# Last stage of a fused four-layer kernel: products turned through VectorE and DRAM in place of TensorE

## The chip, the cores and the metric

The kernel runs on one core of a Trainium2 chip. The metric is the device time of one execution in microseconds, the median of several runs. One further execution was profiled; its trace is what the sections below read.

## The reference

The input x is (16, 128, 512) float32, 2048 rows of 512. Four layers follow one another, each `x = x + tanh(g) * f(layernorm(x))`: a latent cross attention, a feed-forward with routed low-rank parts, a causal attention, and last the layer that the change touches:

```python
h = relu(x @ W1 + b1)
alpha = softmax(h @ W2 + b2)              # 8 weights for each row
vx = einsum('krd,bsd->bskr', V, x)        # 8 x 64 = 512 columns
uvx = einsum('kdr,bskr->bskd', U, vx)
out = einsum('bsk,bskd->bsd', alpha, uvx)
```

All is computed in float32. The products of the last layer are split into a high and a low half (hi, lo) of the type fp32r, and each is three matmuls: lo x hi, hi x lo, hi x hi.

## The kernel before

The rows are worked in four blocks m = 0 to 3 of 512 rows, each of four tiles tb of 128 rows. Every engine runs its own program, written out by hand in the order in which it is to run (functions `tensor`, `scalar`, `vector`, `gpsimd`, `sync`), and the engines meet at semaphores only. An engine that waits holds back all that stands behind it in its program. All transfers are issued from SyncE's program. A function of the same name (`ln_turn`, `out4`, ...) stands in several programs and is the part of that engine in one step.

The steps of the last stage, for block m:

- `h4`: four groups of 12 matmuls, the first layer of the weights. It needs the turned and split rows of the whole block. ScalarE drains each with Relu to H4.
- `logits_a`, `logits_b`: 8 + 8 small matmuls, with a copy by ScalarE (LT) between them; VectorE and ScalarE make the softmax weights `al` of the block.
- `vx4(m, tb)`: 12 matmuls give the 512 columns of vx for a tile. VectorE multiplies them by the weights into VX, which has two buffers.
- `turn4(m, tb)`: four transposes of VX on TensorE (128x128 each, by a product with the identity) into a PSUM bank; ScalarE writes the high half and VectorE the low half to VT4, two buffers.
- `out4(m, tb)`: 12 matmuls by U; VectorE multiplies by tanh(g) and adds x, which lies in X4 (eight buffers); SyncE stores the tile.
- `ln_turn(3, m+1, tb)`: four transposes of the normalised rows of the next block, then the high half by ScalarE and the low half by VectorE. `ln_pre` (statistics, VectorE), the reciprocal root (GpSimd) and `ln_norm` (VectorE) precede it.

TensorE's order in block m before is: h4(m), out4(m-1, 2), logits_a, out4(m-1, 3), logits_b, ln_turn(3, m+1, 0), then for tb = 0 to 4: vx4(m, tb), turn4(m, tb-1), ln_turn(3, m+1, tb), out4(m, tb-2). So behind the last ln_turn of a block stand out4(m, 1) and turn4(m, 3), and then h4(m+1). In block 0 there is no out4 ahead and ln_turn(3, 1, 0) stands in the loop. The rows of the next block are loaded once into X4, where the statistics read them and the sum of out4 is formed later; `ln_norm` writes the normalised rows to XR, a ring of five buffers.

The first stage already turns its attention weights in the way that the change uses: VectorE transposes 32x32 blocks from Pb to PY, SyncE stores PY to a DRAM buffer (`p_store`) and loads it back with the blocks in their places (`p_load`, four loads), then ScalarE and VectorE split it.

Names in the profile go by the memory that a tile lies in: P is P3 (H4, VX), PTV is X4, MSK is LT, AR or XT is the turned rows (XT in even blocks, AR in odd ones) and AR is VT4 and the weights. L118 is a matmul, L121 a transpose on TensorE, L124 an operation of ScalarE, L130 a tensor-tensor and L137 a tensor-scalar one on VectorE, L140 the scaled sum, L164 VectorE's 32x32 transpose, L170 a transfer.

Of the kernel before, what the change touches and what calls it, by code (L numbers as in the profile page):

```python
# [180 lines left out]
def build(nc, i, out):  # L181
    ctx = ExitStack()
    with ctx:
# [123 lines left out]
        VX = P3[:, 1, 0:1024].rearrange("p (b n) -> p b n", b=2)  # L307
        VT4 = ar(0, 2048).rearrange("p (b n) -> p b n", b=2)
# [4 lines left out]
        scr = [nc.dram_tensor(f"scr{k}", [NT, D], F32, kind="Internal").ap() for k in range(3)]  # L313
        pscr = [nc.dram_tensor(f"pscr{k}", [128, 1024], F32, kind="Internal").ap() for k in range(2)]
# [31 lines left out]
        t_py, d_pz = sig("t_py", 16), sig("d_pz", 16)  # L346

# [8 lines left out]
        py_ok, pz_ok = kinds(on_dve, "py_ok pz_ok")  # L356
# [170 lines left out]
        def tensor(pe):  # L527
# [537 lines left out]
            def out4(m, tb):  # L1065
                k = ps.take(("o4", m, tb), ring8.next())
                pe.wait_ge(*ps.free(("o4", m, tb)))
                pe.wait_ge(*ps.drained(("vt", m, tb)))
                pe.wait_ge(*w4_ok["U", 3])
                for c in range(4):  # L1070
                    s, s2 = slice(128 * c, 128 * c + 128), slice(512 + 128 * c, 640 + 128 * c)
                    ins = mm3(k[:, :], (VT4[:, tb % 2, s], VT4[:, tb % 2, s2]), (h3(U4[0], c), h3(U4[1], c)), c == 0, c == 3)
                ins.then_inc(*ps.fill(("o4", m, tb)))

            for m in range(NM):
                more = m + 1 < NM
                if m:
                    h4(m, range(4), ring8)
                    out4(m - 1, 2)
                    logits_a(m)  # L1080
                    out4(m - 1, 3)
                    logits_b(m)
                    if more:
                        ln_turn(3, m + 1, 0, ring8.next())
                for tb in range(5):
                    if tb < 4:
                        vx4(m, tb)
                    if tb >= 1:
                        turn4(m, tb - 1)
                    if more and tb < 4 and (tb >= 1 or m == 0):  # L1090
                        ln_turn(3, m + 1, tb, ring8.next())
                    if 2 <= tb < 4:
                        out4(m, tb - 2)
# [4 lines left out]
        def scalar(ac):  # L1098
# [340 lines left out]

            for m in range(NM):  # L1440
                more = m + 1 < NM
                if m:
                    h4(m, range(4))
                logits(m)
                if m and more:
                    ln_turn(3, m + 1, 0)
                ac.wait_ge(*al_in[m])
                ac.act(al[:, :, :], al[:, :, :], ACT.Exp).then_inc(*al_ex.mark(m))
                for tb in range(5):
                    if tb >= 1:  # L1450
                        turn4(m, tb - 1)
                    if more and tb < 4 and (tb >= 1 or m == 0):
                        ln_turn(3, m + 1, tb)


        def vector(ve_):
# [6 lines left out]
            def ln_pre(ph, m, tb):  # L1463
                par = (4 * ph + m) % 2
                if ph == 3 and m:
                    x = X4[:, 4 * (m % 2) + tb, :]
                    e.wait_ge(*d_x4[4 * (m % 2) + tb][m])
                else:
                    x = xr_ap("ln", ph, m, tb)
                    e.wait_ge(*xr_ld("ln", ph, m, tb))  # L1470
                e.bn_stats(st6[:, tb, :], x).then_inc(*on_dve.step())
                e.wait_ge(*on_dve.now())
                e.bn_aggr(mv[:, par, tb, :], st6[:, tb, :]).then_inc(*on_dve.step())
                e.wait_ge(*on_dve.now())
                e.ts(ve[:, par, tb:tb + 1], mv[:, par, tb, 1:2], EPS, None, ALU.add, None).then_inc(*ve_ok.mark((ph, m, tb)))

            def ln_norm(ph, m, tb):
                par = (4 * ph + m) % 2
                o = xr_ap("ln", ph, m, tb)
                x = X4[:, 4 * (m % 2) + tb, :] if ph == 3 and m else o  # L1480
                e.wait_ge(*rs_ok[ph, m, tb])
                if ph == 3 and m:
                    e.wait_ge(*xr_free("ln", ph, m, tb))
                e.ts(o, x, mv[:, par, tb, 0:1], rstd[:, par, tb:tb + 1], ALU.subtract,
                     ALU.mult).then_inc(*xn_ok.mark((ph, m, tb)))
# [431 lines left out]
            def vx4(m, tb, a):  # L1917
                key = "vx", m, tb
                t = 4 * m + tb
                e.wait_ge(*ps.full(key))  # L1920
                e.wait_ge(*a)
                e.wait_ge(*(ps.full(("vt", (t - 2) // 4, (t - 2) % 4)) if t >= 2 else ps.full(("pt3", 15, 3))))
                e.tt(VX[:, tb % 2, :].rearrange("p (k r) -> p k r", k=8), ps.ap(key)[:, :].rearrange("p (k r) -> p k r", k=8),
                     bc(al[:, tb, :], 64), ALU.mult).then_inc(*ps.drain(key, on_dve))

# [15 lines left out]
            for m in range(NM):  # L1941
                more = m + 1 < NM
                if more and m:
                    ln_pre(3, m + 1, 0)
                    ln_pre(3, m + 1, 1)
                    ln_norm(3, m + 1, 0)
                    ln_norm(3, m + 1, 1)
                if m:
                    out4(m - 1, 2)
                    out4(m - 1, 3)  # L1950
                    a = logits(m)
                    if more:
                        ln_turn(3, m + 1, 0)
                if m == 0:
                    ln_pre(3, 1, 0)
                    ln_pre(3, 1, 1)
                for tb in range(5):
                    if more and tb < 4 and (tb >= 2 or m == 0):
                        ln_norm(3, m + 1, tb)
                    if tb < 4:  # L1960
                        vx4(m, tb, a)
                    if tb >= 1:
                        turn4(m, tb - 1)
                    if more and tb < 4 and (tb >= 1 or m == 0):
# [3 lines left out]
                    if 2 <= tb < 4:  # L1968
# [170 lines left out]
        def sync(e):  # L2139
# [210 lines left out]
            xf_load(3, 3)  # L2350
            x4_load(1)
# [8 lines left out]
            x4_load(0)  # L2360
            for m in range(NM):
                if m and m + 1 < NM:
                    n = 4 * ((m + 1) % 2)
                    for tb in (0, 1):
                        e.wait_ge(*t_x4[n + tb][m - 1])
                        e.wait_ge(*stored(3, m + 1, tb))
                        e.dma(X4[:, n + tb, :], rows(3, m + 1, tb)).then_inc(*d_x4[n + tb].mark(m + 1))
                if m:
                    x4_store(m - 1, 2)
                    x4_store(m - 1, 3)  # L2370
                if m and m + 1 < NM:
                    n = 4 * ((m + 1) % 2)
                    for tb in (2, 3):
                        e.wait_ge(*t_x4[n + tb][m - 1])
                        e.wait_ge(*stored(3, m + 1, tb))
                        e.dma(X4[:, n + tb, :], rows(3, m + 1, tb)).then_inc(*d_x4[n + tb].mark(m + 1))
                x4_store(m, 0)
                x4_store(m, 1)
# [109 lines left out]
```

## Time and profile before

| | us |
|---|---|
| median of 3 runs (lowest, highest) | 1394.04 (1393.75, 1394.27) |
| the profiled execution | 1391.57 |
| its span, first to last instruction | 1389.8 |
| mean granted clock of TensorE | 0.996 |

PE is TensorE's matmuls and PEld its weight loads, which overlap them. DVE is VectorE, ACT ScalarE, POOL GpSimd, SPq the transfers as SyncE issues them. A row of the timeline gives the start, the duration, the engine, the line, the operation, the tile written and the tiles read, and in brackets how long the engine had been idle and who released it. The duration of a matmul or of an operation of VectorE or ScalarE includes its pipeline, so that the next one on the engine starts before the end. The last stage, from the first vx4 on, runs from 1246 us to the end of the span.

### The profile page before, as it was taken

The page shows a single profiled execution, that of the slowest core. Times are in us where ns is not written, and L with a number is a line of the kernel's source. Part 1 is how long each engine was busy: PE and PEld are TensorE (multiplying, and loading weights), DVE is VectorE, ACT ScalarE, POOL GpSimd, SP SyncE. Part 2 cuts the span into 40 slices and gives each one's busy share as a digit, 9 for nine tenths or more (in the row PEclk, how much of TensorE's full clock was granted, in tenths as well). Part 3 has the DMA queues.
Part 4 walks back from the last instruction along what each step waited for, and adds up shares of the span by engine and source line. Part 5 has one row for each costly group of instructions (what it writes and reads, how often), then busy time and mean ns, then how long its engine had stood idle before and what let it go on. Part 6 is the DMA issues. An engine that isn't in the chain of part 4 may idle for free.

```text
span 1389.8 us, 20437 instructions
## 1 busy us (share of the span) xinstructions
PE 1360.6 (98%) x7708; PEld 1103.3 (79%) x7708; DVE 906.3 (65%) x1759; ACT 518.9 (37%) x1569; POOL 416.0 (30%) x463
## 2 busy tenths in 40 slices
PE   7899999999999999999999999999999999999999
PEld 5688888888788788878887888788886788878887
DVE  5566565666674777786677657776888777834443
ACT  2444455454464232231113111311127777712221
POOL 3112423223254352111120111013518865530000
PEclk9999999999999999999999999999999999999999
DMA  7643444433444222110111101111224031131111
GB/s 264 185 153 114 149 124 129 144 107 119 154 147 111 80 76 57 54 38 20 31 46 31 42 23 45 36 46 56 80 82 137 33 114 62 58 116 57 53 46 46
DMA packets 86726, 120.51 MB, mean 87 GB/s; under 512 B 10444, under 2 KB 49484, under 8 KB 86628
## 3 DMA queue, kind: packets, MB, share of 16 engines
q1 hardware_dynamic: 86628, 119.21, 27.4%
q8 instruction: 61, 1.00, 0.3%
q14 instruction: 37, 0.30, 0.1%
HBM read 86.67 MB, written 32.51 MB: 86 GB/s over the span
## 4 chain that ended last, share of the span: by engine, by line
PE 88%; DVE 7%; ACT 2%; DMA 1%; issue 1%; POOL 1%; SPq 1%; DVEq 0%; ACTq 0%
PE bank L118 84%; PE bank L121 5%; DVE XR L140 1%; ACT Pb L124 1%; DVE STG L130 1%; DVE AH L130 1%; SPq L170 1%; DMA PYZ<-pscr 1%; DVE PYZ L164 0%; DVE XR L137 0%; DVE st L152 0%; ACT STG L124 0%; DVE sm L146 0%; DVE AH L127 0%; DMA XR<-in_x_dram 0%
## 5 line engine op out<-in xcount | busy, mean ns | idle before, releaser
L118 PE MATMUL bank<-XT,AR 128*128 128x512 f32 x1152 | 280.2, 393 | 0.3 <-DVE AR L130 0.2
L118 PE MATMUL bank<-AR 128*128 128x512 f32 x1056 | 262.3, 397 | 5.8 <-DVE Msb L127 4.9
L118 PEld LDWEIGHTS bank<-XT,AR 128*128 128x128 f32 x1152 | 213.8, 188 | 48.4 <-issue 1.5
L118 PEld LDWEIGHTS bank<-AR 128*128 128x128 f32 x1056 | 193.7, 188 | 52.2 <-DVE Msb L127 5.3
L124 ACT ACTIVATE STG<-bank,b1c 128x512 f32<-128x512 f32 x128 | 88.4, 690 | 379.1 <-PE bank L118 302.7
L118 PE MATMUL bank<-AR,CT 128*128 128x512 f32 x768 | 194.2, 396 | 1.8 <-DVE CT L130 1.8
L118 PE MATMUL bank<-AR,AH 128*128 128x512 f32 x768 | 187.6, 391 | 0.0
L127 DVE CAST AH<-STG 128x512 fp32r<-128x512 f32 x192 | 90.5, 471 | 120.9 <-PE bank L118 106.6
L118 PEld LDWEIGHTS bank<-AR,AH 128*128 128x128 f32 x768 | 143.0, 188 | 30.4 <-issue 1.1
L118 PEld LDWEIGHTS bank<-AR,CT 128*128 128x128 f32 x768 | 141.1, 190 | 30.1 <-DVE CT L130 2.5
L127 POOL CAST BA<-STG 128x256 fp32r<-128x256 f32 x64 | 29.7, 464 | 422.2 <-PE bank L118 321.1
L130 DVE TENSOR_TENSOR AH<-STG,AH 128x512 fp32r<-128x512 f32 x192 | 142.6, 743 | 6.6
L124 ACT ACTIVATE Pb<-bank,sm 128x128 f32<-128x128 f32 x256 | 90.1, 377 | 118.0 <-DVE sm L136 118.0
L130 POOL TENSOR_TENSOR Pb<-Pb,sm 128x512 f32<-128x512 f32 x64 | 66.6, 1042 | 189.5 <-DVE sm L149 189.5
L118 PE MATMUL bank<-TM,BA 128*128 128x512 f32 x384 | 107.7, 392 | 0.5 <-ACT STG L124 0.4
L124 ACT ACTIVATE P<-bank,sm 128x128 f32<-128x128 f32 x256 | 90.1, 395 | 31.9 <-DVE sm L146 31.9
L130 POOL TENSOR_TENSOR rstd<-ve,mhalf 128x1 f32<-128x1 f32 x64 | 48.1, 755 | 170.3 <-DVE ve L136 170.2
L118 PE MATMUL bank<-AH,BA 128*128 128x512 f32 x384 | 98.0, 390 | 0.0
L130 DVE TENSOR_TENSOR STG<-STG 128x512 f32<-128x512 f32 x128 | 89.9, 702 | 4.2
L130 POOL TENSOR_TENSOR P<-P,sm 128x512 f32<-128x512 f32 x64 | 65.4, 1042 | 82.1 <-DVE sm L149 82.0
L124 ACT ACTIVATE AR<-bank 128x512 fp32r<-128x512 f32 x88 | 51.7, 603 | 100.2 <-PE bank L121 75.2
L118 PEld LDWEIGHTS bank<-TM,BA 128*128 128x128 f32 x384 | 71.3, 188 | 17.6 <-ACT STG L124 2.2
(135 smaller groups left out, 1860.1 us busy)
## 6 DMA issues: line engine op xcount, KB each, us to landing
pscr<-PYZ SPq DMA_DIRECT2D x30, 512.0 KB, 2.9
PYZ<-pscr SPq DMA_DIRECT2D x120, 128.0 KB, 3.0
XR<-scr SPq DMA_DIRECT2D x52, 256.0 KB, 2.8
XR<-in_x_dram SPq DMA_DIRECT2D x32, 256.0 KB, 4.0
scr<-XR SPq DMA_DIRECT2D x32, 256.0 KB, 2.7
STG<-in_Wq_dram SPq DMA_DIRECT2D x8, 512.0 KB, 5.4
STG<-in_WoT_dram SPq DMA_DIRECT2D x8, 512.0 KB, 6.1
STG<-in_W1L_dram SPq DMA_DIRECT2D x16, 256.0 KB, 2.6
```

The source lines that it names most:

```text
L118: return self.e.matmul(o, w, x, start=start, stop=stop, skip_group_check=True) if self.e else Nothing()
L121: return self.e.transpose(o, x, ident) if self.e else Nothing()
L124: return self.e.activation(o, x, func, **kw) if self.e else Nothing()
L127: return self.e.tensor_copy(o, x) if self.e else Nothing()
L130: return self.e.tensor_tensor(out=o, in0=a, in1=b, op=op) if self.e else Nothing()
L140: return self.e.scalar_tensor_tensor(out=o, in0=a, scalar=s, in1=b, op0=op0, op1=op1) if self.e else Nothing()
L170: return self.e.dma_start(o, x) if self.e else Nothing()
```

## The change

In blocks 0 to 2 the weighted products are no longer turned by TensorE. VectorE transposes their 32x32 blocks into a new buffer VY (`blocks4`), SyncE stores the tile to DRAM (`v_store`) and loads it back into XF with the blocks in their places (`v_back`, four loads of 64 KB), and ScalarE and VectorE split it from there to VT4 (`split4`). The four out4 of a block now stand in the next block: behind h4, between logits_a and logits_b, and the last two behind ln_turn(3, m+1, 0). The splits stand in the programs of ScalarE and VectorE between the other steps of that block. Block 3 keeps turn4. The rows of the blocks 1 to 3 are loaded twice, into XR for the layer norm and into X4 for the sum, and `ln_norm` works in place in XR.

```diff
--- before.py
+++ after.py
@@ -305,12 +305,14 @@
         U4 = (ar(14336, 2048), ar(16384, 2048))
         E4 = (ar(18432, 2048), ar(20480, 2048))
         VX = P3[:, 1, 0:1024].rearrange("p (b n) -> p b n", b=2)
+        VY = P3[:, 1, 1024:2048].rearrange("p (b n) -> p b n", b=2)
         VT4 = ar(0, 2048).rearrange("p (b n) -> p b n", b=2)
         H4 = P3[:, 0, :].rearrange("p (c n) -> p c n", c=4)
         X4 = PTV[:, :].rearrange("p (n d) -> p n d", n=8)
         LT = MSK[:, 0, :]
 
         scr = [nc.dram_tensor(f"scr{k}", [NT, D], F32, kind="Internal").ap() for k in range(3)]
+        vscr = [nc.dram_tensor(f"vscr{k}", [128, 512], F32, kind="Internal").ap() for k in range(2)]
         pscr = [nc.dram_tensor(f"pscr{k}", [128, 1024], F32, kind="Internal").ap() for k in range(2)]
         xs = [i["x"], scr[0], scr[1], scr[2], out]
 
...
@@ -1065,7 +1069,7 @@
             def out4(m, tb):
                 k = ps.take(("o4", m, tb), ring8.next())
                 pe.wait_ge(*ps.free(("o4", m, tb)))
-                pe.wait_ge(*ps.drained(("vt", m, tb)))
+                pe.wait_ge(*(vz_ok[m, tb] if m < 3 else ps.drained(("vt", m, tb))))
                 pe.wait_ge(*w4_ok["U", 3])
                 for c in range(4):
                     s, s2 = slice(128 * c, 128 * c + 128), slice(512 + 128 * c, 640 + 128 * c)
@@ -1076,20 +1080,22 @@
                 more = m + 1 < NM
                 if m:
                     h4(m, range(4), ring8)
-                    out4(m - 1, 2)
+                    out4(m - 1, 0)
                     logits_a(m)
-                    out4(m - 1, 3)
+                    out4(m - 1, 1)
                     logits_b(m)
                     if more:
                         ln_turn(3, m + 1, 0, ring8.next())
-                for tb in range(5):
+                    out4(m - 1, 2)
+                    out4(m - 1, 3)
+                for tb in range(4 if more else 5):
                     if tb < 4:
                         vx4(m, tb)
-                    if tb >= 1:
+                    if not more and tb >= 1:
                         turn4(m, tb - 1)
-                    if more and tb < 4 and (tb >= 1 or m == 0):
+                    if more and (tb >= 1 or m == 0):
                         ln_turn(3, m + 1, tb, ring8.next())
-                    if 2 <= tb < 4:
+                    if not more and 2 <= tb < 4:
                         out4(m, tb - 2)
             out4(NM - 1, 2)
             out4(NM - 1, 3)
@@ -1437,19 +1443,33 @@
                 ac.wait_ge(*(ps.full(("o4", (t - 2) // 4, (t - 2) % 4)) if t >= 2 else ps.full(("w3", 3, 3))))
                 hi_of(key, VT4[:, tb % 2, 0:512], ps.ap(key)[:, :])
 
+            def split4(m, tb):
+                t = 4 * m + tb
+                ac.wait_ge(*d_vz[tb][m, 3])
+                ac.wait_ge(*(ps.full(("o4", (t - 2) // 4, (t - 2) % 4)) if t >= 2 else ps.full(("w3", 3, 3))))
+                hi_of(("vz", m, tb), VT4[:, tb % 2, 0:512].rearrange("p (n j c) -> p n j c", n=4, j=4),
+                      XF[:, tb, :].rearrange("p (j n c) -> p n j c", j=4, n=4))
+
             for m in range(NM):
                 more = m + 1 < NM
                 if m:
-                    h4(m, range(4))
+                    split4(m - 1, 0)
+                    h4(m, (0, 1))
+                    split4(m - 1, 1)
+                    h4(m, (2, 3))
                 logits(m)
                 if m and more:
                     ln_turn(3, m + 1, 0)
+                if m:
+                    split4(m - 1, 2)
                 ac.wait_ge(*al_in[m])
                 ac.act(al[:, :, :], al[:, :, :], ACT.Exp).then_inc(*al_ex.mark(m))
-                for tb in range(5):
-                    if tb >= 1:
+                if m:
+                    split4(m - 1, 3)
+                for tb in range(4 if more else 5):
+                    if not more and tb >= 1:
                         turn4(m, tb - 1)
-                    if more and tb < 4 and (tb >= 1 or m == 0):
+                    if more and (tb >= 1 or m == 0):
                         ln_turn(3, m + 1, tb)
 
 
@@ -1462,12 +1482,8 @@
 
             def ln_pre(ph, m, tb):
                 par = (4 * ph + m) % 2
-                if ph == 3 and m:
-                    x = X4[:, 4 * (m % 2) + tb, :]
-                    e.wait_ge(*d_x4[4 * (m % 2) + tb][m])
-                else:
-                    x = xr_ap("ln", ph, m, tb)
-                    e.wait_ge(*xr_ld("ln", ph, m, tb))
+                x = xr_ap("ln", ph, m, tb)
+                e.wait_ge(*xr_ld("ln", ph, m, tb))
                 e.bn_stats(st6[:, tb, :], x).then_inc(*on_dve.step())
                 e.wait_ge(*on_dve.now())
                 e.bn_aggr(mv[:, par, tb, :], st6[:, tb, :]).then_inc(*on_dve.step())
@@ -1477,11 +1493,8 @@
             def ln_norm(ph, m, tb):
                 par = (4 * ph + m) % 2
                 o = xr_ap("ln", ph, m, tb)
-                x = X4[:, 4 * (m % 2) + tb, :] if ph == 3 and m else o
                 e.wait_ge(*rs_ok[ph, m, tb])
-                if ph == 3 and m:
-                    e.wait_ge(*xr_free("ln", ph, m, tb))
-                e.ts(o, x, mv[:, par, tb, 0:1], rstd[:, par, tb:tb + 1], ALU.subtract,
+                e.ts(o, o, mv[:, par, tb, 0:1], rstd[:, par, tb:tb + 1], ALU.subtract,
                      ALU.mult).then_inc(*xn_ok.mark((ph, m, tb)))
 
             def ln_turn(ph, m, tb):
@@ -1919,9 +1932,23 @@
                 t = 4 * m + tb
                 e.wait_ge(*ps.full(key))
                 e.wait_ge(*a)
-                e.wait_ge(*(ps.full(("vt", (t - 2) // 4, (t - 2) % 4)) if t >= 2 else ps.full(("pt3", 15, 3))))
+                if t >= 14:
+                    e.wait_ge(*ps.full(("vt", 3, tb - 2)))
+                else:
+                    e.wait_ge(*(vy_ok[(t - 2) // 4, (t - 2) % 4] if t >= 2 else ps.full(("pt3", 15, 3))))
                 e.tt(VX[:, tb % 2, :].rearrange("p (k r) -> p k r", k=8), ps.ap(key)[:, :].rearrange("p (k r) -> p k r", k=8),
                      bc(al[:, tb, :], 64), ALU.mult).then_inc(*ps.drain(key, on_dve))
+
+            def blocks4(m, tb):
+                t = 4 * m + tb
+                e.wait_ge(*ps.drained(("vx", m, tb)))
+                e.wait_ge(*(t_vy[tb % 2][t - 2] if t >= 2 else ps.full(("pt3", 15, 3))))
+                e.turn(blocks_out(VY[:, tb % 2, :]), blocks_in(VX[:, tb % 2, :])).then_inc(*vy_ok.mark((m, tb)))
+
+            def split4(m, tb):
+                lo_of(("vz", m, tb), VT4[:, tb % 2, 512:1024].rearrange("p (n j c) -> p n j c", n=4, j=4),
+                      XF[:, tb, :].rearrange("p (j n c) -> p n j c", j=4, n=4),
+                      VT4[:, tb % 2, 0:512].rearrange("p (n j c) -> p n j c", n=4, j=4)).then_inc(*vz_ok.mark((m, tb)))
 
             def turn4(m, tb):
                 key = "vt", m, tb
@@ -1940,32 +1967,40 @@
                 final3(3, b)
             for m in range(NM):
                 more = m + 1 < NM
-                if more and m:
-                    ln_pre(3, m + 1, 0)
-                    ln_pre(3, m + 1, 1)
-                    ln_norm(3, m + 1, 0)
-                    ln_norm(3, m + 1, 1)
                 if m:
-                    out4(m - 1, 2)
-                    out4(m - 1, 3)
+                    split4(m - 1, 0)
+                    split4(m - 1, 1)
+                    if more:
+                        ln_pre(3, m + 1, 0)
+                        ln_pre(3, m + 1, 1)
+                        ln_norm(3, m + 1, 0)
+                        ln_norm(3, m + 1, 1)
+                    out4(m - 1, 0)
+                    split4(m - 1, 2)
+                    out4(m - 1, 1)
                     a = logits(m)
                     if more:
                         ln_turn(3, m + 1, 0)
+                    split4(m - 1, 3)
+                    out4(m - 1, 2)
+                    out4(m - 1, 3)
                 if m == 0:
                     ln_pre(3, 1, 0)
                     ln_pre(3, 1, 1)
-                for tb in range(5):
-                    if more and tb < 4 and (tb >= 2 or m == 0):
+                for tb in range(4 if more else 5):
+                    if more and (tb >= 2 or m == 0):
                         ln_norm(3, m + 1, tb)
                     if tb < 4:
                         vx4(m, tb, a)
-                    if tb >= 1:
+                    if more:
+                        blocks4(m, tb)
+                    elif tb >= 1:
                         turn4(m, tb - 1)
-                    if more and tb < 4 and (tb >= 1 or m == 0):
+                    if more and (tb >= 1 or m == 0):
                         ln_turn(3, m + 1, tb)
                     if more and tb < 2:
                         ln_pre(3, m + 1, tb + 2)
-                    if 2 <= tb < 4:
+                    if not more and 2 <= tb < 4:
                         out4(m, tb - 2)
             out4(NM - 1, 2)
             out4(NM - 1, 3)
@@ -2348,6 +2383,8 @@
                 for block in wo_at(u):
                     xf_store(*block)
             xf_load(3, 3)
+            for tb in range(4):
+                ln_load(3, 1, tb)
             x4_load(1)
             for tb in range(4):
                 xf_store(3, tb)
@@ -2358,24 +2395,45 @@
                 e.dma(rows(4, m, tb), X4[:, n, :]).then_inc(*t_x4[n].mark(m))
 
             x4_load(0)
+
+            def v_store(m, tb):
+                t = 4 * m + tb
+                e.wait_ge(*vy_ok[m, tb])
+                if t >= 2:
+                    e.wait_ge(*d_vz[(t - 2) % 4][(t - 2) // 4, 3])
+                e.dma(vscr[tb % 2], VY[:, tb % 2, :]).then_inc(*t_vy[tb % 2].mark(t))
+
+            def v_back(m, tb):
+                t = 4 * m + tb
+                e.wait_ge(*t_vy[tb % 2][t])
+                e.wait_ge(*(vz_ok[m - 1, tb] if m else t_xf[tb][3]))
+                src = vscr[tb % 2].rearrange("(j r) (i x) -> i r j x", j=4, i=4)
+                for k in range(4):
+                    e.dma(XF[32 * k:32 * k + 32, tb, :].rearrange("r (j x) -> r j x", j=4), src[k]).then_inc(
+                        *d_vz[tb].mark((m, k)))
+
             for m in range(NM):
-                if m and m + 1 < NM:
-                    n = 4 * ((m + 1) % 2)
-                    for tb in (0, 1):
-                        e.wait_ge(*t_x4[n + tb][m - 1])
-                        e.wait_ge(*stored(3, m + 1, tb))
-                        e.dma(X4[:, n + tb, :], rows(3, m + 1, tb)).then_inc(*d_x4[n + tb].mark(m + 1))
+                more = m + 1 < NM
+                if m and more:
+                    for tb in range(4):
+                        ln_load(3, m + 1, tb)
                 if m:
-                    x4_store(m - 1, 2)
-                    x4_store(m - 1, 3)
-                if m and m + 1 < NM:
-                    n = 4 * ((m + 1) % 2)
-                    for tb in (2, 3):
-                        e.wait_ge(*t_x4[n + tb][m - 1])
-                        e.wait_ge(*stored(3, m + 1, tb))
-                        e.dma(X4[:, n + tb, :], rows(3, m + 1, tb)).then_inc(*d_x4[n + tb].mark(m + 1))
-                x4_store(m, 0)
-                x4_store(m, 1)
+                    for tb in range(4):
+                        n = 4 * ((m - 1) % 2) + tb
+                        x4_store(m - 1, tb)
+                        if more:
+                            e.wait_ge(*t_x4[n][m - 1])
+                            e.wait_ge(*stored(3, m + 1, tb))
+                            e.dma(X4[:, n, :], rows(3, m + 1, tb)).then_inc(*d_x4[n].mark(m + 1))
+                if more:
+                    for tb in range(4):
+                        v_store(m, tb)
+                        if tb:
+                            v_back(m, tb - 1)
+                    v_back(m, 3)
+                else:
+                    x4_store(m, 0)
+                    x4_store(m, 1)
             x4_store(NM - 1, 2)
             x4_store(NM - 1, 3)
             for n in range(8):
```

The signals and counters that the new steps use (`t_vy`, `d_vz`, `vy_ok`, `vz_ok`) are declared where the dots stand.

## Rows read from the trace of the kernel before

**Rows 1.** The page: busy time, share of the span and instructions of each engine.
```profile
PE 1360.6 (98%) x7708; PEld 1103.3 (79%) x7708; DVE 906.3 (65%) x1759; ACT 518.9 (37%) x1569; POOL 416.0 (30%) x463
```

**Rows 2.** Busy time in two windows: blocks 0 and 1; PEclk is the granted clock.
```profile
1246.00:1267.00 21.00, 20.34 (x105) 16.71 (x104) 14.19 (x29) 3.89 (x7) 2.91 (x4) 1.00 0.23 78
1267.00:1305.60 38.60, 38.60 (x197) 31.41 (x195) 17.94 (x39) 7.94 (x14) 2.67 (x4) 1.00 0.17 56
```

**Rows 3.** Waits from 1246 to 1345: us in total, times, longest.
```profile
PE bank L121 <- DVE XR L137: 0.7, 1, 0.7
```

**Rows 4.** The chain that ended last: start, us; turn4(1, 2) and ln_turn(3, 2, 3).
```profile
1301.77 0.87 PE bank L121 x8
```

**Rows 5.** Timeline, end of block 1: vx4(1, 3), ln_turn(3, 2, 3), h4(2).
```profile
1301.81 0.69 DVE L130 TENSOR_TENSOR P<-bank,al 128x512 f32<-128x512 f32 x1 [1.52 <-PE bank L118]
...
1302.05 0.60 PE L121 MATMUL bank<-ident,XR 128*128 128x128 f32 x4
...
1302.74 0.59 ACT L124 ACTIVATE XT<-bank 128x512 fp32r<-128x512 f32 x1
...
1303.49 0.68 DVE L130 TENSOR_TENSOR XT<-bank,XT 128x512 fp32r<-128x512 f32 x1
...
1305.58 1.41 PE L118 MATMUL bank<-XT,AR 128*128 128x512 f32 x5
```

**Rows 6.** Timeline, block 1: out4(0, 3), ln_turn(3, 2, 0) and the softmax weights.
```profile
1285.08 0.75 DVE L140 SCALAR_TENSOR_TENSOR PTV<-bank,tg,PTV 128x512 f32<-128x512 f32 x1 [3.20 <-PE bank L118]
...
1285.62 0.64 PE L121 MATMUL bank<-ident,XR 128*128 128x128 f32 x4
1285.80 0.19 DVE L130 TENSOR_TENSOR al<-bank,b 128x32 f32<-128x32 f32 x1
...
1286.25 0.19 DVE L130 TENSOR_TENSOR al<-al,s 128x32 f32<-128x32 f32 x1
1286.29 0.60 ACT L124 ACTIVATE XT<-bank 128x512 fp32r<-128x512 f32 x1 [3.61 <-PE bank L121]
1286.79 0.22 ACT L124 ACTIVATE al<-al 128x32 f32<-128x32 f32 x1
...
1287.58 0.68 DVE L130 TENSOR_TENSOR XT<-bank,XT 128x512 fp32r<-128x512 f32 x1
```

**Rows 7.** Timeline, blocks 0 and 1: vx4(0, 1), the norms, turn4(0, 0).
```profile
1250.28 3.00 PE L118 MATMUL bank<-AR,XT 128*128 128x512 f32 x12
...
1252.80 0.54 DVE L137 TENSOR_SCALAR XR<-PTV,mv,rstd 128x512 f32<-128x512 f32 x1
...
1253.12 0.60 PE L121 MATMUL bank<-ident,P 128*128 128x128 f32 x4
...
1293.43 0.68 DVE L130 TENSOR_TENSOR XT<-bank,XT 128x512 fp32r<-128x512 f32 x1
1294.03 0.68 DVE L152 BATCH_NORM_STATS2 st<-PTV 128x6 f32<-128x512 f32 x1
...
1295.04 0.54 DVE L137 TENSOR_SCALAR XR<-PTV,mv,rstd 128x512 f32<-128x512 f32 x1
```

**Rows 8.** Line 137, norms in place: ns min/median/max, first and last start.
```profile
L137 DVE TENSOR_SCALAR XR<-XR,mv,rstd x36: 503/540/1575, 11.8 to 1010.6; 128x512 f32<-128x512 f32 x36
```

**Rows 9.** Tile PYZ of the first stage: turning, splits, time to landing.
```profile
L164 DVE STREAM_TRANSPOSE PYZ<-Pb x60: 662/686/708, 40.5 to 412.6; 128x512 f32<-128x512 f32 x60
...
L124 ACT ACTIVATE PT<-PYZ x30: 1050/1062/1067, 54.8 to 423.7; 128x1024 fp32r<-128x1024 f32 x30
L130 DVE TENSOR_TENSOR PT<-PYZ,PT x30: 1214/1225/1450, 55.9 to 424.8; 128x1024 fp32r<-128x1024 f32 x30
...
DMA to landing us min/median/max: 2.4/2.9/7.6
```

**Rows 10.** SyncE's issues in the first stage: one store and its four loads.
```profile
402.00 0.34 SPq L170 DMA_DIRECT2D pscr<-PYZ  x1
404.92 1.75 SPq L170 DMA_DIRECT2D PYZ<-pscr  x4
```

More of the change, by code:

```diff
@@ L346, in build @@
         t_py, d_pz = sig("t_py", 16), sig("d_pz", 16)
+        t_vy = [sig(f"t_vy{k}", 16) for k in range(2)]
+        d_vz = [sig(f"d_vz{k}", 16) for k in range(4)]
         def kinds(count, names):
@@ L355, in build @@
         ms2_ok, tl_ok2, tl_sum, al_in, ix_ok = kinds(on_dve, "ms2_ok tl_ok2 tl_sum al_in ix_ok")
-        py_ok, pz_ok = kinds(on_dve, "py_ok pz_ok")
+        vy_ok, vz_ok, py_ok, pz_ok = kinds(on_dve, "vy_ok vz_ok py_ok pz_ok")
         c_mh, c_sel, rs_ok, kvc_rd, kvr_ok, kvl_ok = kinds(on_pool, "c_mh c_sel rs_ok kvc_rd kvr_ok kvl_ok")
```

## The prediction

> **What bounds the kernel.** The page first: TensorE is busy for 98% of the span [rows 1]. The windows over the last stage show the same in the three blocks that the change touches (38.60 of 38.60 us in block 1), at a granted clock of 1.00 [rows 2]. The list of waits there has one wait of TensorE on another engine, 0.7 us for the first normalised rows [rows 3]. So this stage has no slack: an instruction taken from TensorE is gained in full, and a wait put in front of it is lost in full. VectorE (14.2 of 21 us in block 0), ScalarE and the transfers have room on average. What counts is the moment at which they deliver.
>
> I write H for the start of a block's first-layer products h4, F for the end of a block's last (or named) vx product group, L for the start of the transposes ln_turn(3, m+1, 0) on TensorE.
>
> **Removed.** Twelve groups of four transposes turn4 (blocks 0 to 2, four each). By the chain, two groups in a row cost 0.87 us, so one costs 0.43 [rows 4]. 12 x 0.43 = 5.2 us less.
>
> **Output products moved.** out4(m,0) and (m,1) stood between the vx groups and now stand behind the next h4. Their number is the same; that costs nothing in itself. But out4(m,1), with turn4(m,3) behind it, lay between ln_turn(3, m+1, 3) and h4, and h4 needs these last turned rows. Row by row in block 1 [rows 5]: last vx matmul ends at F = 1301.77 [rows 4], the transposes start at F-0.16, at 1302.05 only because turn4 stood ahead. ScalarE's half starts 0.04 after they end, VectorE's half 0.03 after that; all was done at 1304.17, 1.4 us before h4 at 1305.58. That cover is gone. New: transposes F-0.16 to F+0.44; ScalarE F+0.48 to F+1.08. VectorE starts vx4(m,3) at F+0.04, then the added blocks4(m,3): an operation of 0.68 or 0.69 holds VectorE for 0.60 before the next starts (1293.43 to 1294.03 [rows 7]); the turning one takes 0.69 [rows 9], for which I take 0.61, with the full 0.69 as the other bound, so the lo half starts at F+1.25 and ends at F+1.93; h4 starts at F+1.98 instead of F+0.23. Loss 1.75 us at the end of each of blocks 0, 1, 2: **5.25 us**.
>
> **Splits inside block m.** For m = 1 and 2 ScalarE's order is now LT copy, ln_turn(3, m+1, 0), split4(m-1, 2), Exp, split4(m-1, 3); on TensorE out4(m-1, 2) follows ln_turn(3, m+1, 0) at once. So behind the transposes at L stand two ScalarE operations and one of VectorE before out4(m-1, 2) may start. ScalarE takes the turned rows at L+0.67 (1286.29 against 1285.62), the next operation starts 0.50 later (1286.79) [rows 6], L+1.17. The split reads and writes 512 columns in blocks of 32; the trace has it only at 1024 columns, 1.06 on ScalarE and 1.23 on VectorE [rows 9]. Bounds: half of these (0.53, 0.61), and the two times of the 512-column split out of PSUM (0.59, 0.68 [rows 5]); I take the upper pair, which has this size. ScalarE L+1.17 to L+1.77, VectorE L+1.80 to L+2.50, TensorE starts at L+2.55 where it would have started at L+0.40. Loss 2.15.
> Next: out4(m-1, 2) keeps TensorE until L+5.39 (12 matmuls take 2.84, 1250.28 to 1253.12 [rows 7]). VectorE goes on after split 2 with out4(m-1, 1) at L+2.42, logits at L+3.14 (0.72 behind, as 1285.80 to 1285.08), Exp can start when its input is there, 0.67 later, at L+3.81. The turned-row lo half started 1.78 after the logits' first operation, of which 0.32 was Exp waiting for its turn (1286.44 to 1286.79, less the 0.03 of a hand-over) [rows 6], so L+4.61 now, then split4(m-1, 3) L+5.21 to L+5.91 and out4(m-1, 3) at L+5.96. Loss 0.6. Together **2 x 2.75 = 5.5 us**. In block 3 there is no ln_turn: split 2 follows the LT copy, some 3 us ahead of its product, and nothing is lost.
>
> **Normalised rows.** In blocks 1 and 2, VectorE between F of vx4(m,1) and the norm of rows 2: vx 0.64 with its hand-over, blocks4 0.61, lo half 0.61, ln_pre 1.01 (1294.03 to 1295.04) and the norm 0.54 [rows 7] end at F+3.40. TensorE wants them after vx4(m,2), 0.23+2.84 = 3.07 after F, now that no turn4 and no other product stands between. Loss 0.4 each. In block 0 the norm of rows 1 ended at 1253.34, as it will again (nothing ahead of it on VectorE gets slower: blocks4 falls under ScalarE's half), and TensorE arrives at 1253.12 [rows 7]: 0.3, and for rows 2 0.2. Together **1.3 us**. The 0.7 of [rows 3] stays: what VectorE does ahead of it is unchanged. The norm itself now runs in place in XR; the 36 in-place cases have a median of the same 0.54 [rows 8].
>
> **Through DRAM.** Per tile: VectorE's turning 0.69, one store, four loads. Store to the issue of the loads took 2.92 us (402.00 to 404.92) [rows 10], the four issues 1.75, landing 2.9 in the median and 7.6 at most [rows 9]. The last of four lands 1.31+2.9 = 4.2 after the first issue. SyncE stores tile t only when tile t-2 is back, so from vy1 (VectorE done with tile 1) the loads have landed at vy1+4.6, +9.3, +14.0, +16.5, and H is at vy1+7.7 in block 0 (vy1 = 1254.6, H = 1262.3). Splits 0 and 1 are wanted by their products at H+11 and H+15, and ScalarE reaches them at H and H+6; 2 and 3 after H+19. All are in time by 3 us or more. Behind them in SyncE's queue stand the four loads of the rows for the next layer norm: issued at about vy1+14, landed at H+10, normed by H+13, wanted on TensorE at H+18.5. Also free. The stores and loads of X4 now alternate in one queue, each load behind the landing of a store; the last leaves 2 us before v_store(m, 0) is due. VectorE's 12 turnings (0.61 each, 7.3 us) cost nothing beyond the steps above. Rows loaded twice are 12 transfers of 256 KB on queues with a DMA share of 0.17 to 0.23 [rows 2]: nothing.
>
> **Sum.** -5.2 + 5.25 + 5.5 + 1.3 = +6.9 us. The profiled execution took 1391.57 us (span 1389.8 and 1.8 around it), which becomes 1398.5; the median of the runs stands 2.5 above it at 1394.04, and becomes **1400.9**. Not in the sum: a restarted TensorE may show a weight load of 0.19 at each of 11 waits, +2.1; the lower bounds of the split, four times 0.07, and an earlier blocks4 take off about 1. With a little more late data that is 1398 to 1405.
>
> **Rivals.**
> A, faster: the waits are covered after all and only the transposes count. It would need hand-overs on both sides to fit into about 0.4 us instead of 2.0 and 2.5: -5.2+1.3 = -3.9, 1390.1. It decides as soon as all waits add up to under 5.2. For it speaks that ScalarE and VectorE have idle time all along; against it that each step is an in-order dependence with a duration in a row. 4%.
> B, no change: the wait ahead of h4 comes, but the one inside the block doesn't (ScalarE gets to split 2 before the transposes). -5.2+5.25+1.3 = +1.4, 1395.4. Against: the order written for ScalarE. 5%.
> C, the way through DRAM is late: every load lands after 7.6. Then each tile takes 9.3 in the queue, loads for split 2 land at H+20 and the rows of the next norm are normed at H+21 instead of before 18.5: about 3 us more in three blocks, 1411. For: one landing of that length; against: the median of 120 is 2.9. 4%.
> D: the loads that turn blocks by stride are far slower than plain ones. If a tile's return cost some 15 us instead of 4.2, the queue holds split 2 back to H+38, where its product would start at H+21 otherwise, 17 us in three blocks, 1450. The trace has 120 such loads with pieces of 1 KB, landing in 2.9, so 1%. The Trainium skill ("VectorE: DVE Perf Modes", the three transpose paths) warns that a plain DMA copy doing a transpose by strides is 19 times slower than the DMA's own transpose path when the innermost destination stride is large; the innermost runs here are contiguous (512 bytes), so its case isn't this one.
> The forecast has 86%. Within 0.2% is 2.8 us, about what a measurement can tell from no change: slower 0.91, same 0.05, faster 0.04.
>
> **What would show it.** After: no transposes with P as input but 16 in block 3; TensorE waits for VectorE's XT/AR half ahead of h4, three of about 1.75 us, and ahead of out4(m-1, 2) two of about 2.15 and (m-1, 3) two of 0.6; DVE turning rows VY at 0.69, twelve; ScalarE hardly ever waiting on the DMA for XF. I am wrong if the waits ahead of the products name the DMA (then C), or if the largest wait of TensorE in the stage is under 1 us (A).

## The result and the profile after

The changed kernel takes 1403.49 us (1402.45 to 1404.84, four runs), the kernel before beside it 1394.11: a ratio of 1.007, 95% interval 1.0058 to 1.0082, or 9.4 us more. The forecast was 1400.9, within 1398 to 1405.

The profiled execution took 1402.45 us, its span 1400.7. The page's busy times, as in [rows 1]:
```profile
PE 1362.0 (97%) x7660; PEld 1100.8 (79%) x7660; DVE 914.8 (65%) x1771; ACT 518.4 (37%) x1569; POOL 415.2 (30%) x463
```
The 48 transposes are gone (7708 to 7660), and yet TensorE isn't busy for less time: 1362.0 us against 1360.6, and over the last stage alone 139.8 us in both kernels (windows 1246 to 1390 before, 1247 to 1401 after). That is the first sign of something that the forecast lacked: some of the same matmuls have become slower. The windows over blocks 0 and 1 (they answer to [rows 2]; the last three figures are granted clock, DMA share, GB/s):
```profile
1247.00:1263.40 16.40, 13.86 (x67) 10.48 (x65) 14.40 (x30) 2.92 (x5) 2.90 (x4) 1.00 0.50 165
1263.40:1306.40 43.00, 39.02 (x177) 30.75 (x177) 20.16 (x43) 8.05 (x14) 2.66 (x4) 0.96 0.38 122
```
Block 1 had no idle time on TensorE before; now it has 4 us, and a mean clock of 0.96. The waits of the stage, as in [rows 3], with the weight loads left out:
```profile
PE bank L118 <- DVE AR L130: 7.2, 4, 1.9
...
PE bank L118 <- DVE XT L130: 1.7, 1, 1.7
PE bank L121 <- DVE XR L137: 1.4, 3, 0.7
```
Read the buffers, not only the engine: AR is both the turned rows of odd blocks and VT4, XT the turned rows of even blocks. Two waits of 1.9 are for VT4, three of 1.7 for turned rows, the rest for normed rows. None names a transfer.

The end of block 1, the timeline that answers to [rows 5]:
```profile
1304.11 0.60 PE L121 MATMUL bank<-ident,XR 128*128 128x128 f32 x4
1304.31 0.69 DVE L130 TENSOR_TENSOR P<-bank,al 128x512 f32<-128x512 f32 x1 [1.00 <-PE bank L118]
1304.74 0.60 ACT L124 ACTIVATE XT<-bank 128x512 fp32r<-128x512 f32 x1 [2.61 <-PE bank L121]
1305.03 0.71 DVE L164 STREAM_TRANSPOSE P<-P 128x512 f32<-128x512 f32 x1
...
1305.67 0.65 DVE L130 TENSOR_TENSOR XT<-bank,XT 128x512 fp32r<-128x512 f32 x1
...
1306.38 0.50 PE L118 MATMUL bank<-XT,AR 128*128 128x512 f32 x1 [1.67 <-DVE XT L130]
```
ScalarE is done at 1305.34, but VectorE's half starts only at 1305.67 behind the added turning. TensorE is due 0.35 after 1304.11, at 1304.46, and starts at 1306.38: 1.9 late, of which 1.67 show as idle behind the transposes' pipeline.

Inside block 1, around ln_turn(3, 2, 0), the timeline that answers to [rows 6]:
```profile
1281.96 0.64 PE L121 MATMUL bank<-ident,XR 128*128 128x128 f32 x4
1282.63 0.60 ACT L124 ACTIVATE XT<-bank 128x512 fp32r<-128x512 f32 x1 [3.61 <-PE bank L121]
1283.12 0.62 ACT L124 ACTIVATE AR<-XF 128x512 fp32r<-128x512 f32 x1
1283.78 0.69 DVE L130 TENSOR_TENSOR AR<-XF,AR 128x512 fp32r<-128x512 f32 x1 [5.55 <-ACT AR L124]
...
1284.52 12.76 PE L118 MATMUL bank<-AR 128*128 128x512 f32 x48 [1.93 <-DVE AR L130]
```
The forecast had ScalarE's split at L+1.17, VectorE's at L+1.80 and TensorE at L+2.55; it is L+1.16, +1.82, +2.56. But the 48 matmuls that follow take 12.76 us, where the 48 of h4(2), behind the wait above, take 11.22. Windows over the same place show why; the last two rows are from block 2, where the same matmuls start at 1327.47:
```profile
1283.00:1284.50 1.50, 0.00 (x0) 0.00 (x0) 0.72 (x2) 0.74 (x2) 0.00 (x0) 1.00 0.01 3
1284.50:1285.00 0.50, 0.48 (x1) 0.48 (x2) 0.50 (x1) 0.00 (x0) 0.00 (x0) 0.51 0.00 0
1285.00:1286.00 1.00, 1.00 (x4) 0.71 (x4) 0.64 (x5) 0.29 (x2) 0.00 (x0) 0.50 0.01 2
...
1288.00:1289.00 1.00, 1.00 (x6) 0.80 (x5) 0.00 (x0) 0.00 (x0) 0.00 (x0) 1.00 0.48 158
...
1327.40:1328.00 0.60, 0.53 (x2) 0.48 (x3) 0.60 (x3) 0.00 (x0) 0.00 (x0) 1.00 0.00 0
...
1329.00:1330.00 1.00, 1.00 (x4) 0.80 (x3) 0.93 (x4) 0.40 (x1) 0.00 (x0) 0.50 0.66 246
```
In block 1 the granted clock is at 0.50 (1.2 of 2.4 GHz) from the restart until about 1287.9. VectorE starts draining out4(0, 2) at 1289.21:
```profile
1289.21 0.75 DVE L140 SCALAR_TENSOR_TENSOR PTV<-bank,tg,PTV 128x512 f32<-128x512 f32 x1 [1.42 <-PE bank L118]
```
That is 4.69 us after the product's first matmul; vx4(0, 1), at full clock in the kernel before, had 3.04 (1250.28 to 1253.32). So the slow stretch costs 1.65 us by the drains, and 1.54 by the two groups of 48. The forecast wait of 0.6 ahead of out4(0, 3) lies inside it. Block 2 has the same wait of 1.93 and is as long as block 1, but there the clock falls only 1.4 us after the restart: it is at 0.50 from 1328.9 to 1332.3.

The way through DRAM, as it is now:
```profile
L164 DVE STREAM_TRANSPOSE P<-P x12: 711/711/712, 1251.4 to 1348.0; 128x512 f32<-128x512 f32 x12
```
```profile
DMA to landing us min/median/max: 1.9/2.0/3.6
```
The second line is for the stores of VY and the loads of XF together.

**The sum.** Executions reach this stage at different times, up to 7 us apart, with the same order of work on TensorE ahead of it (1246.3 to 1253.1 in the profiles here). So I compare stage times: from the start of vx4(0, 0) to the start of VectorE's last sum. Each comes from one profiled execution; the one kernel that was profiled twice (e5 below) gave 137.94 and 137.89. Before: 1246.32 to 1386.53, 140.2 us. After: 1247.30 to 1397.41, 150.1 us. Of the 10.9 us between the two spans, 1.0 arose ahead of the stage and 9.9 in it. By the starts of h4: block 0 now 16.1 us (forecast 15.9), blocks 1 and 2 42.95 and 42.96 (41.6), the remainder 48.1 (48.0: the 42.5 of before, plus two products).

### The profile page after: what moved, and what is told of

Read it like the earlier page. It is cut to its first block, busy times and chain, and to the rows that moved or that the text cites. A ratio compares the mean times of both kernels' runs of the same rounds, so it can differ in the third digit from the quotient of the medians.

```text
span 1400.7 us, 20456 instructions
## 1 busy us (share of the span) xinstructions
PE 1362.0 (97%) x7660; PEld 1100.8 (79%) x7660; DVE 914.8 (65%) x1771; ACT 518.4 (37%) x1569; POOL 415.2 (30%) x463
## 4 chain that ended last, share of the span: by engine, by line
PE 86%; DVE 8%; DMA 2%; ACT 2%; issue 1%; SPq 1%; POOL 1%; DVEq 0%; ACTq 0%
PE bank L118 81%; PE bank L121 4%; DMA PYZ<-pscr 1%; SPq L170 1%; DVE XR L140 1%; DVE PYZ L164 1%; DVE AR L130 1%; ACT Pb L124 1%; DVE XR L137 1%; DVE st L152 1%; DVE STG L130 1%; DVE AH L130 0%; DMA pscr<-PYZ 0%; DVE sm L146 0%; ACT PT L124 0%
## 5 line engine op out<-in xcount | busy, mean ns | idle before, releaser
L118 PEld LDWEIGHTS bank<-AH,BA 128*128 128x128 f32 x384 | 71.8, 188 | 15.2
```

The lines of the kernel that those rows point to most:

```text
L118: return self.e.matmul(o, w, x, start=start, stop=stop, skip_group_check=True) if self.e else Nothing()
```

## The experiments

The diffs are against the changed kernel, unless said otherwise. Each profile's stage time is given beside the timed runs.

**e1: ScalarE's order.**
```diff
                 logits(m)
-                if m and more:
-                    ln_turn(3, m + 1, 0)
                 if m:
                     split4(m - 1, 2)
+                if m and more:
+                    ln_turn(3, m + 1, 0)
```


> The changed kernel (1403.5 us) with one edit: on ScalarE split4(m-1, 2) stands ahead of ln_turn(3, m+1, 0) in blocks 1 and 2, instead of behind it. Theory: ScalarE's order makes TensorE wait 1.9 us idle (2.17 from the due start) ahead of out4(m-1, 2); its clock then falls to 0.50 for 3.4 us and out4(m-1, 2) takes 4.45 instead of 2.84, within which the wait for split 3 is hidden. Without the wait neither comes: 2 x (2.17 + 1.65) = 7.6 less, 1395.9 us, and no stretch of the stage below a clock of 1.00. Rival one, the product really waits for the way through DRAM: no change, 1403.5, and the wait names the DMA. Rival two, the slow matmuls come from transfers beside them and not from the wait: only the wait goes, 4.3 less, 1399.2, and out4(m-1, 2) still takes over 4 us.

Measured: 1397.44 us, ratio 1.0024 (1.0014 to 1.0034); stage 142.9 us, 7.2 less (7.6 expected). Blocks 1 and 2 are 39.4 and 39.3 us. The timeline at the same place:
```profile
1287.76 0.64 PE L121 MATMUL bank<-ident,XR 128*128 128x128 f32 x4
...
1288.15 11.37 PE L118 MATMUL bank<-AR 128*128 128x512 f32 x48
```
No idle time behind the transposes, 48 matmuls at full pace, and the mean clock from 1262 to 1395 is 1.00. Two lines swapped on an engine busy 37% of the time are worth three quarters of the stage's loss. Both rivals fall: that of the way through DRAM and that of the transfers beside the matmuls. The runs' 1397.4 is 1.5 above the expected 1395.9; the stage accounts for 0.4 of that, the rest lies ahead of the stage or in the spread of the runs.

**e2: the cover ahead of h4.** A short form of the edit on TensorE, for blocks 1 and 2 (VectorE's sum and SyncE's store and load of that tile move too):
```diff
                     out4(m - 1, 2)
-                    out4(m - 1, 3)
+                    if not more:
+                        out4(m - 1, 3)
...
+                if m and more:
+                    out4(m - 1, 3)
```


> The changed kernel with out4(m-1, 3) of blocks 1 and 2 moved behind ln_turn(3, m+1, 3), the last turned rows, on TensorE and VectorE, and its store and the load behind it moved behind v_back(m, 3) on SyncE. So 12 matmuls of 2.8 us stand again between the turned rows and h4, as in the kernel before. Theory: the wait of 1.75 us ahead of h4 was the lost cover and goes at the ends of blocks 1 and 2, 3.5 less, 1400.0 us; the one at the end of block 0 stays, as there is no older product to put there. The wait ahead of out4(m-1, 2) and its slow matmuls stay. Rival: VectorE is busy from the last vx to h4 and what is covered there comes back as a wait in the h4 groups or at the next product: under 1 us less, 1403.

Measured: 1400.8 us, ratio 1.0051 (1.0035 to 1.0067), an interval that still touches the changed kernel's; stage 146.3 us, 3.8 less. The last turned rows of block 1, out4(0, 3) and h4(2) now follow without a gap:
```profile
1302.27 0.60 PE L121 MATMUL bank<-ident,XR 128*128 128x128 f32 x4
1302.62 3.02 PE L118 MATMUL bank<-AR 128*128 128x512 f32 x12
1305.48 4.70 PE L118 MATMUL bank<-XT,AR 128*128 128x512 f32 x20
```
The lost cover was real and comes back whole. The slow stretch behind the wait for split 2 stays, within out4(0, 2): the mean clock is 0.53 from 1285.4 to 1288.5.

**e3: the wait filled.** Nine matmuls with full operands ahead of TensorE's wait.
```diff
                 pe.wait_ge(*ps.free(("o4", m, tb)))
+                if tb == 2 and m < 2:
+                    for c in range(3):
+                        s = slice(128 * c, 128 * c + 128)
+                        mm3(k[:, :], (E4[0][:, s], E4[1][:, s]), xh(xt_of(3, m + 1), c), True, True)
```


> The changed kernel with nine extra matmuls (128x512, 2.07 us by the trace's pace, results overwritten) on TensorE ahead of its wait for split 2 in blocks 1 and 2: they fill the wait of 2.17 us and take nothing away from it. Theory: the slow out4(m-1, 2) (4.45 us instead of 2.84) follows from the idle time, so with it filled the clock stays at 1.00; the wait for split 3, 0.55, is then seen again. 2 x (1.65 - 0.55) = 2.2 less, 1401.3 us although work is added. Rival, transfers beside these matmuls slow them: they are as slow as before, 1403.5 us.

Measured: stage 148.2 us, 1.95 less; ratio 1.0062 (1.0044 to 1.0079), median 1403.45, so the runs can't tell it from 1.007. The stage can:
```profile
1285.16 0.64 PE L121 MATMUL bank<-ident,XR 128*128 128x128 f32 x4
1285.55 5.19 PE L118 MATMUL bank<-AR 128*128 128x512 f32 x21
1291.06 8.46 PE L118 MATMUL bank<-AR 128*128 128x512 f32 x36 [0.32 <-DVE AR L130]
```
Twelve matmuls of out4(0, 2) and the nine added ones take 5.19 us at a clock of 1.00, then the forecast wait for split 3 is there (0.32 idle), then full pace. With 4.1 us of matmuls added, the stage is 2 us shorter. Its transfers are those of the changed kernel, so they aren't what slows the matmuls: with the wait filled, the slow stretch is gone.

**e8: what came before the wait.** The same nine matmuls between logits_b and ln_turn.
```diff
                     logits_b(m)
                     if more:
-                        ln_turn(3, m + 1, 0, ring8.next())
+                        bank = ring8.next()
+                        k = ps.take(("fill", m), bank)
...
+                            ins = mm3(k[:, :], (E4[0][:, s], E4[1][:, s]), xh(xt_of(3, m), c), True, True)
...
+                        ln_turn(3, m + 1, 0, bank)
```


> The changed kernel with nine extra matmuls of full size (2.07 us, results overwritten) between logits_b and ln_turn(3, m+1, 0) in blocks 1 and 2. The wait of 1.93 us behind the transposes stays. If the fall of the clock after it depends on the small matmuls (16 of the logits, and transposes) that come before, the clock now stays at 1.00 and out4(m-1, 2) takes 2.84 us, a block is 42.95 + 2.07 - 1.06 = 44.0 us. If the idle time alone decides, the 12 matmuls after it are slow again, and a block is 45.0 us.

Measured in a single execution: 1409.84 us, stage 154.4 us, blocks 1 and 2 45.1 us. The clock fell again (windows: the wait, then the restart):
```profile
1287.80:1289.70 1.90, 0.01 (x1) 0.00 (x0) 0.71 (x2) 1.12 (x2) 0.00 (x0) 1.00 0.00 0
1289.80:1293.00 3.20, 3.20 (x9) 2.56 (x10) 2.77 (x9) 0.75 (x2) 0.00 (x0) 0.62 0.22 82
```
So the small matmuls of the logits aren't what brings it on; my idea of them falls.

**e7: rows loaded twice, alone.** The kernel before with only this edit (in `ln_pre` and `ln_norm` as in the change, and on SyncE, where the same four loads for block 1 stand ahead of `x4_load(1)`):
```diff
             for m in range(NM):
+                if m and m + 1 < NM:
+                    for tb in range(4):
+                        ln_load(3, m + 1, tb)
```


> The kernel before with one part of the change alone: the rows of blocks 1 to 3 are loaded a second time, into XR, and normalised in place. Twelve more transfers of 256 KB, and VectorE no longer waits for X4. Theory: this part neither costs nor brings anything, 1394 us, blocks of 38.4 us as before. Rival: the transfers or the fuller SyncE queue are part of the loss, above 1396 us.

Measured: ratio 1.0006 (0.9995 to 1.0017); stage 140.3 us against 140.2. This part is free.

**e5: all covers in blocks 1 and 2.** e1's order, and on TensorE (ln_turn moves in the same way on ScalarE and VectorE, and the norms on VectorE move ahead):
```diff
-                    if more and (tb >= 1 or m == 0):
+                    if more and m == 0:
                         ln_turn(3, m + 1, tb, ring8.next())
+                    elif more and tb < 3:
+                        ln_turn(3, m + 1, tb + 1, ring8.next())
```


> The changed kernel with the order of e1 and, in blocks 1 and 2, the norms of the next block made during the out4 groups and each ln_turn one tile earlier (behind vx4(m, 0), (m, 1), (m, 2) instead of (m, 1), (m, 2), (m, 3)), so that vx4(m, 3) covers the last turned rows. Theory: all waits of blocks 1 and 2 go: 2 x (2.17 + 1.65) + 2 x 1.75 + 2 x 0.4 = 11.9 less, 1391.6 us, some 2.5 below the kernel before; block 0 keeps its waits (2.2 us over before). Rival: VectorE, with 12 turnings more, becomes the bound of the vx4 part and the waits only move: then not below 1394.

Measured: 1391.68 us, ratio 0.9984 (0.9974 to 0.9994); stage 137.9 us, 12.2 less than the changed kernel and 2.3 less than the one before. TensorE's waits that are left in the stage are those of block 0, 0.66 and 1.67 us, so the rival falls: VectorE isn't the bound.

**e6: block 0.** On top of e5:
```diff
-            for b in range(1, 4):
+            for b in range(1, 3):
                 wo3(3, b)
...
+                if m == 0:
+                    wo3(3, 3)
```


> The kernel of e5 with the attention layer's last output product, w3(3, 3), moved on TensorE from ahead of vx4(0, 0) to behind ln_turn(3, 1, 3), at the end of block 0; its sum on VectorE and its store on SyncE (ahead of v_back(0, 3)) move with it. Theory: block 0's wait of 1.75 us ahead of h4(1) is the same lost cover as in blocks 1 and 2 and any product of 2.8 us fills it; the wait for the first normalised rows becomes some 0.3 shorter. 2.0 less than e5's 1391.7, 1389.7 us. Rival: block 0 is bound by VectorE, which was ready only just in time for each ln_turn; then starting 2.8 us earlier gives waits there in place of the one removed, and the time stays at 1391.7.

Measured: 1390.8 us, ratio 0.9987 (0.9977 to 0.9997), which can't be told from e5. The stage, with the 2.8 us of the product that was moved into it taken off, is 135.9 us, 2.0 less than e5. TensorE no longer waits ahead of h4(1):
```profile
1262.30 0.44 PE bank L121 x4
1262.73 21.11 PE bank L118 x100
```
That is the chain that ended last: 12 matmuls of w3(3, 3) and h4 and its followers without a break. The wait for the first normed rows stayed at 0.66, where I had expected 0.3 less: VectorE's chain to it moved forward exactly as far as TensorE did.

**e9 and e5 again.** On top of e6, in VectorE's block 0:
```diff
                     if tb < 4:
                         vx4(m, tb, a)
+                    if m == 0 and tb < 3:
+                        ln_norm(3, 1, tb + 1)
```


> The kernel of e6_block0 with the norms of block 1's rows one step earlier in VectorE's order of block 0: ln_norm(3, 1, tb+1) directly behind vx4(0, tb), ahead of blocks4(0, tb). Theory: of block 0's remaining waits the first (0.66 us, the first normalised rows) stays and the two of 0.5 us ahead of ln_turn(3, 1, 1) and (3, 1, 2) go, 1.0 less than e6_block0 and 3.0 less than e5_all in this stage. Rival: VectorE has 3.3 us of work in each of these steps against 3.2 on TensorE, so the waits move to the next turn: no gain over e6_block0.

> The same kernel as e5_all, beside e9_norms0 on the same chip: 1391.7 us, a ratio of 0.9984 to the kernel before, if its gain is real; within 0.05% of the kernel before if it was chance. e9_norms0 should then stand 3.0 us below it.

Measured side by side: e9 1389.48 us, ratio 0.9969 (0.9958 to 0.998); e5 again 1392.23, 0.9989 (0.9976 to 1.0001), which includes no change: e5's gain over the kernel before rests on its stage time. The two stand 2.75 us apart (3.0 expected). e9's stage is 135.2 us, 0.7 less than e6 (1.0 expected), 2.7 less than e5 and 5.0 less than before. In its stage only the first wait of TensorE remains:
```profile
PE bank L121 <- DVE XR L137: 0.7, 1, 0.7
```
By its ratio e9 is 4.3 us faster than the kernel before, clear of its interval.

## Why the prediction came out as it did

- **Transposes removed, 5.2 us: right, by two ways.** The losses, counted from the due start, are 3 x 1.9 ahead of h4, 2 x 2.17 and 2 x 1.65 at split 2, and 1.6 for the norms, 14.9 together; the stage lost 9.9, which leaves 5.0 for the gain. And e9, where all added waits are gone, is 5.0 below the kernel before in the stage.
- **Lost cover ahead of h4, 3 x 1.75: right in its cause, small by 0.15 each.** Measured 1.67 of idle time, 1.9 from the due start; e2 took two of them away, and 3.8 us with them, e6 the third.
- **Wait for split 2, 2.15: right to 0.02** in each of its terms; e1 shows ScalarE's order as the cause. The trace before had this split only at twice the size; 0.62 and 0.69 were measured where 0.60 and 0.70 had been taken.
- **Wait for split 3, 0.6: the step that was mis-sized.** It is there once the clock is kept up (e3), but in the changed kernel TensorE runs at half clock for 3.4 us behind its restart, which costs 1.65 and hides this wait: 2 x 1.05 = 2.1 of the 3.0 us by which the stage exceeds the forecast (1.9 with the 1.54 of the other reading). I had put nothing on what an idle stretch does to TensorE's clock: the granted clock in [rows 2] was 1.00, in blocks with next to no idle time. The trace of the kernel before did have it elsewhere, and I had drawn nothing from it:
```profile
458.95 1.19 PE L118 MATMUL bank<-TM,SEL 24*128 24x512 f32 x4 [1.39 <-DVE TM L130]
460.07 4.61 PE L118 MATMUL bank<-AR,CT 128*128 128x512 f32 x12
```
Behind waits of 0.62 and 1.39 us these 12 matmuls take 4.61 us where 12 take 3.0 in [rows 7], and the granted clock is at 0.50 from 460.9 to 464.3.
- **Norms, 1.3: right in its cause**, some 1.6 by the rows. The rest of the excess, 0.9 us, is mostly VectorE's added turning, at the h4 waits and here. The rows at the end of block 1 show it: the turning starts 0.72 after vx4's operation (1304.31 to 1305.03), as it waits for that one's result, where the forecast let the next operation start after 0.60; and it holds VectorE for 0.64 (to 1305.67), not 0.61. So the lo half starts 1.36 after vx4's operation, not 1.21, and this is the 1.9 against 1.75. The 2.1 that the forecast had for restarts, outside its sum, isn't seen.
- **Through DRAM: right that it is free, too dear in its parts.** Landing took 2.0 us, not 2.9, with loads of half the size; ScalarE waited for a load nowhere in the changed stage. The turning lasts 0.71, not 0.69.
- **The number.** The measured 1403.5 lies within 1398 to 1405, but that is in part luck: the room above 1400.9 was meant for restarts and late data, and the clock filled it.
- **Rivals.** A needed all the waits to stay away, B those inside the blocks; both kinds came. C and D needed late transfers; the longest landing was 3.6 us.

On the sentence cited from the Trainium skill in rival D (VectorE: DVE Perf Modes, the three transpose paths): the runs agree that its case isn't this one, as 48 loads with strided blocks and 512-byte runs landed in a median of 2.0 us together with the stores, and never over 3.6. No run here timed the DMA's own transpose path.

## What to carry to other kernels

On an engine that is never idle, taking work away gives its full time, but a product that stood between a hand-over and its user is worth the length of the hand-over (here 1.9 us) as cover, whatever else it does: before moving one, list what it covers, and put another in its place. In an in-order program check, for every operation that an engine gets in addition, what now stands ahead of it; here one line in ScalarE's order was worth 7 of 10 us. And price a wait on TensorE at its length plus what the matmuls after it lose, until a run has shown the clock.

## What the runs showed of the hardware

The clock fell to 0.50 after each of the six waits of 1.93 us idle ahead of out4(m-1, 2) (two each in the changed kernel, e2 and e8). The slow stretch began 0 to 1.4 us after the restart, lasted some 3.4 us each time, and cost 1.5 to 1.65 us where it could be read off. After the waits of 1.67 us ahead of h4 the clock stayed at 1.00, in all fifteen of them (three each in the changed kernel, e1, e3 and e8, one each in e2 and the two profiles of e5), as here at the end of block 2 of the changed kernel:
```profile
1348.00:1349.30 1.30, 0.00 (x0) 0.00 (x0) 1.30 (x3) 0.82 (x2) 0.00 (x0) 1.00 0.77 260
1349.30:1350.00 0.70, 0.66 (x3) 0.56 (x4) 0.58 (x1) 0.00 (x0) 0.00 (x0) 1.00 0.58 164
```
Both kinds of wait follow four transposes. e8 excludes the small matmuls of the logits, e3 the transfers; no run changed the length of either wait alone. But the length of one wait doesn't decide by itself. Near the start of the kernel TensorE waits 2.38 us for the first normalised rows in the kernel before (2.02 in the changed one), and no window there shows less than 1.00. And the waits of 0.6 and 1.39 us near 460 us, with a short group of transposes between them, are in every profile: in ten of the eleven the clock fell behind them, and in e9 it stayed at 1.00 and the same 12 matmuls ran at full pace:
```profile
461.84 3.01 PE L118 MATMUL bank<-AR,CT 128*128 128x512 f32 x12
```
So the same stretch of a program can keep or lose its clock from one execution to the next, and what decides it stays open.
